# A flamingo block (gated cross-attention, then a mixture of experts) on one core: the last batch's softmax sums moved by fp32 products, routing waits and tables rearranged

## What is computed

```python
x = x + tanh(g_xattn[0]) * xattn(layernorm(x), ctx, Wq, bq, Wk, bk, Wv, bv, Wo, bo)
x = x + tanh(g_ffn[0]) * ffn(layernorm(x), gate_w, w1, w2, w3)
# xattn: q, k, v = W @ x + b over channels; per head softmax(q k * SCALE) v; then Wo @ out + bo
# ffn:   logits = x @ gate_w.T; top 2 of softmax; sum of w2 (silu(w1 x) * (w3 x)) * weight
```

## Time and profile before

| | us |
|---|---|
| median of 3 runs (775.40 to 776.07) | 775.88 |
| the profiled execution's own time | 774.61 |
| its span, first to last instruction | 772.9 |

### The profile page before, as it was taken

One profiled execution on the slowest core, in us unless ns is written; L12 is line 12 of the kernel. 1 busy time (PEld: TensorE's weight loads), 2 busy tenths in 40 slices (PEclk: granted clock), 3 DMA queues, 4 the chain that ended last, 5 costly groups with the idle time before them and its releaser, 6 DMA issues.

```text
span 772.9 us, 14065 instructions
## 1 busy us (share of the span) xinstructions
PE 636.8 (82%) x4313; PEld 298.2 (39%) x4314; DVE 414.1 (54%) x765; ACT 328.7 (43%) x395; POOL 227.0 (29%) x176
## 2 busy tenths in 40 slices
PE   8397599998989999899774130399999999999992
PEld 6321022322323233233112020366666666666661
DVE  5464658577695867766394555753333343334330
ACT  2076468576766857677761000022222222222220
POOL 3321124123242231421010020523334445444331
PEclk9789689899998999999986555599999999999997
DMA  7739668587776868868677636737777777755433
GB/s 248 243 105 348 187 196 282 160 286 244 227 231 195 291 193 265 271 188 277 203 221 221 201 117 237 260 107 190 199 200 190 190 196 210 197 105 92 82 42 42
DMA packets 64436, 153.44 MB, mean 199 GB/s; under 512 B 8261, under 2 KB 13894, under 8 KB 62854
## 3 DMA queue, kind: packets, MB, share of 16 engines
q1 hardware_dynamic: 44848, 98.58, 37.9%
q0 software_dynamic: 9632, 22.55, 15.4%
q10 hardware_dynamic: 9910, 31.75, 13.3%
HBM read 92.04 MB, written 58.46 MB: 195 GB/s over the span
## 4 chain that ended last, share of the span: by engine, by line
PE 43%; DMA 25%; DVE 13%; issue 8%; SPq 5%; POOL 4%; ACT 1%; POOLq 0%; DVEq 0%; ACTq 0%
PE S L1463 16%; PE O L1484 9%; DMA weight_parts<-wp 8%; DMA residual<-x 5%; PE O L1318 4%; DMA out<-yo,slot_out 4%; DMA q_parts<-qs 3%; PE S L1279 3%; PE MA L1358 2%; DVE wp L877 2%; PE S L1450 2%; PE MA L1379 2%; DMA zl<-osum 2%; PE MC L1358 2%; DVE wp L879 2%
## 5 line engine op out<-in xcount | busy, mean ns | idle before, releaser
L769 ACT ACTIVATE prob<-S 128x1024 f32<-128x1024 f32 x256 | 254.2, 1025 | 144.7 <-PE S L1279 113.1
L1463 PE MATMUL S<-W,xT 128*128 x1032 | 148.7, 301 | 1.2 <-DVE xT L1219 1.2
L1318 PE MATMUL O<-prob,V 128*32 128x512 f32 x1024 | 147.4, 650 | 0.0
L1279 PE MATMUL S<-Q,K 48*128 48x512 f16 x512 | 101.5, 411 | 35.4 <-ACT prob L769 25.3
L1463 PEld LDWEIGHTS S<-W,xT 128*128 128x128 f16 x1032 | 99.6, 98 | 38.4 <-issue 1.4
L687 POOL DMA_INDIRECT out<-yo,slot_out x43 | 68.6, 1594 | 119.5 <-ACT yo L819 78.8
L1279 PEld LDWEIGHTS S<-Q,K 48*128 48x128 f16 x512 | 24.0, 94 | 182.3 <-ACT prob L769 110.8
L1484 PE MATMUL O<-W,hT 128*128 (+1 forms) x344 | 90.3, 381 | 0.9 <-DVE hT L1239 0.9
L1227 DVE SCALAR_TENSOR_TENSOR hh<-S,act 128x320 f32<-128x320 f32 x43 | 21.1, 492 | 122.0 <-PE S L1463 122.0
L879 DVE SCALAR_TENSOR_TENSOR wp<-wf,wp 128x1024 f16<-128x1024 f32 x48 | 69.7, 1452 | 1.7
L877 DVE TENSOR_SCALAR wp<-wf 128x1024 f16<-128x1024 f32 x48 | 41.4, 862 | 37.4 <-DMA weight_parts<-wp 37.4
(11 more groups left out here) (171 smaller groups left out, 675.5 us busy)
## 6 DMA issues: line engine op xcount, KB each, us to landing
wf<-wall ACTq DMA_DIRECT2D x48, 512.0 KB, 6.5
weight_parts<-wp SPq DMA_DIRECT2D x46, 512.0 KB, 7.3
W<-weight_parts SPq DMA_DIRECT2D x10, 2048.0 KB, 10.1
K<-k_parts SPq DMA_DIRECT2D x8, 1024.0 KB, 11.7
Q<-q_parts SPq DMA_DIRECT2D x8, 1024.0 KB, 7.7
k_parts<-ks SPq DMA_DIRECT2D x24, 256.0 KB
q_parts<-qs SPq DMA_DIRECT2D x24, 256.0 KB
ctx<-ctx_in SPq DMA_DIRECT2D x8, 512.0 KB, 8.2
```

The costliest lines, as they stand in the source:

```text
L769: act.activation(prob[:, u % RING, :], S[u % 2][:, :], ACT.Exp, scale=SCALE).then_inc(g.exp, 1)
L1279: last = pe.matmul(S[u % 2][:, s * T:(s + 1) * T], K[par][r0:r0 + rows_, 2 * g4 + n, st * P:(st + 1) * P], Q[par][r0:r0 + rows_, 2 * g4 + ...
L1318: last = pe.matmul(O[g4 % 2][2 * DK * j:2 * DK * (j + 1), :], V[par][:, st, head(g4, j), :], prob[:, u % RING, (j % 2) * T:(j % 2 + 1) * T ...
L1463: last = pe.matmul(ps, xT[par][:, xp * TT + k, :], W[:, bass.ds(off + (w * WCOL + (2 * k + n) * F), F)], start=(k == 0 and (xp, w) == (0, 0)),
```

## The change

It does six things.

1. For batch 7 alone, the sums no longer go through DRAM. POOL writes four 0/1 matrices into the idle tile `cs` in slot 8 (`pick`, one memset and four copies). PE multiplies `osum` by them: DEN spreads the sums over their values' rows, NUM moves the second half of the values (`shared`; two fp32 products of 128x512 each). For the first half of the channels (m=0) the sums are spread at step 11 of slot 8, into MA; DVE inverts all 512 columns at once and `over_sums` moves the values by four smaller DMAs. For m=1 both products run at the start of slot 9, into S0. The bounds are still tested on `zl`, which four small DMAs now fill.
2. The logits of batch 6 move from step 15 of slot 8 to slot 9, behind these products; the best two of 12 groups are taken in slot 8, of four after `both_runs`. `bad` is made after batch 7's product; PE waits for it before o1. In slot 9 statistics, inverse spread and normed x go half by half, and the two copies to `xT2` stand ahead of the fp16 part of x.
3. In all slots the first half of `lg` waits only for the copy of t0, and its second half for t1.
4. Quarters: five in slots 6 and 7 (a new one at step 9), nine in slot 8 (none at 7 and 11, one at 14), one in slot 9, four in FFN tiles.
5. DVE no longer waits for PE's `s_done` nor for the store of the tokens (POOL waits for that). ACT and SP wait, for each expert, only for its own quarters; ACT's wait for `osum` ends with slot 8's DMAs.
6. The weighted tables are made by DVE: the first behind `row_hot`, the second behind `table`. The FFN loop writes out 7 tiles instead of 3 ahead of its rounds.

```diff
@@ quarters @@
+        STEPS = {0: (), 1: (1, 3, 5, 7, 9, 11, 13, 14), 2: (2, 7, 12, 14),
+                 3: (2, 7, 12, 14), 4: (2, 7, 12, 14), 5: (2, 7, 12, 14),
+                 6: (2, 7, 9, 12, 14), 7: (2, 7, 9, 12, 14), 8: (0, 2, 4, 6, 9, 10, 12, 13, 14),
+                 9: (2,)}
-            elif t.i is None and t.add == B:
-                steps = (0, 2, 4, 6, 7, 9, 10, 11, 12, 13)
-            elif t.i is None and t.add == B + 1:
-                steps, first = (2, 2, 10, 10), At(None, 0, QUARTERS - 6)
@@ tiles @@
-            first = TR - 1
+            first = 2 * TR - 1
@@ sync: slot @@
-                    if c:
-                        bc = t.before(2)
+                    bc = t.before(2)
+                    if c and not b_:
+                        wait(sp, g.os, bc, GROUPS, GROUPS)
+                        last_sums(1)
+                    elif c:
...
-                    else:
+                    elif b_:
                         weights(0, 9)
+                        sp.wait_ge(g.os, GROUPS * (B - 1) + 2)
+                        sp.wait_ge(g.on, B)
+                        last_sums(0)
+                        weights(9, 10)
...
+                        if b_ and not a:
+                            sp.wait_ge(g.zl, 16 * (B + 1))
+                            sp.wait_ge(g.shared, 1)
+                            for j in range(GH):
+                                over_sums(j, osum[1 - par], 1)
+                            weights(10, 13)
                         wait(sp, g.x2l, bc, 1, 1, s_bog)
...
-                    weights(10 if a else 9, VS)
+                    weights(10 if a else 13 if b_ else 0, VS)
@@ scalar: experts 0 and 1 @@
-                act.wait_ge(g.oz, OZ * B + 16)
+                act.wait_ge(g.oz, OZ * (B - 1) + OZ_LAST + 16)
...
-            for n in range(2):
-                act.wait_ge(s_wst[n], 16 * (2 * NE - 1))
             for e in range(EB // 2):
+                for n in range(2):
+                    act.wait_ge(s_wst[n], 16 * 2 * (e + 1))
@@ vector: the last slot @@
+                def last_normed():
+                    of = osum[(B - 1) % 2]
+                    dve.wait_ge(g.oz, OZ * (B - 1) + OZ_LAST + 16)
+                    dve.wait_ge(g.rz, B)
+                    dve.tensor_tensor(on[:, 0, :], of[:, 0, :], zc[:, 0, :], ALU.mult).then_inc(g.rz, 1)
+                    dve.wait_ge(g.rz, B + 1)
+                    dve.tensor_copy(os_[:, 0, 0, :], on[:, 0, :]).then_inc(g.rz, 1)
+                    dve.wait_ge(g.rz, B + 2)
+                    dve.tensor_tensor(os_[:, 1, 0, :], on[:, 0, :], os_[:, 0, 0, :], ALU.subtract).then_inc(g.rz, 1)
+                    dve.wait_ge(g.shared, 2)
+                    dve.reciprocal(zc[:, 1, :], S[0][:, 0:T]).then_inc(g.rz, 1)
+                    if not guard:
+                        dve.wait_ge(g.zl, 16 * (B + 3))
+                        bounds(At(None, 0, B - 1))
...
+                    dve.wait_ge(g.shared, 3)
+                    dve.wait_ge(g.rz, B + 4)
+                    dve.tensor_tensor(on[:, 1, :], S[0][:, T:2 * T], zc[:, 1, :], ALU.mult).then_inc(g.on, 1)
+                    dve.wait_ge(g.c_full, NCU * (B - 1))
+                    logits_out(At(None, 0, B - 2))
...
+                        if last_b and v == DEN_AT:
+                            dve.wait_ge(g.shared, 1)
+                            dve.reciprocal(zc[:, 0, :], MA[:, :]).then_inc(g.rz, 1)
+                            best(g.best, 0, NT - 2 * CT)
@@ vector: routing @@
-            dve.sem_inc(s_done, 1)
-            dve.wait_ge(s_done, 2)
-            best(s_best, NT - CT, NT)
+            best(s_best, NT - 2 * CT, NT)
...
+            weighted(0, w_hi)
             dve.wait_ge(s_tab, 1)
...
+            weighted(1, w_lo)
             dve.wait_ge(s_tab, 2)
...
-                if j.i is None and j.add < 2:
+                if j.i is None and j.add < 4:
-                    split_quarter(At(None, 0, QUARTERS - 2 + j.add))
+                    split_quarter(At(None, 0, QUARTERS - 4 + j.add))
@@ tensor @@
-                    wait(pe, g.c_free, b, NCU, 1 + {"o0": 0, "o1": 0, "t0": 1, "t1": 2, "lg": 4}[name])
+                    wait(pe, g.c_free, b, NCU, 1 + {"o0": 0, "o1": 0, "t0": 1, "t1": 2, "lg": 3}[name])
...
                         for m in range(CT):
+                            wait(pe, g.c_free, b, NCU, C_USES["t0"] + 2 + m)
...
+                def shared(into, of0, of1, m):
+                    pe.wait_ge(g.sel, 5)
+                    for n, of in enumerate((of0, of1)):
+                        pe.wait_ge(g.os, GROUPS * (B - 1) + 2 * m + 1 + n)
+                        last = pe.matmul(into, picked(of), osum[(B - 1) % 2][:, CT * n + m, :], start=(n == 0), stop=(n == 1))
+                    last.then_inc(g.shared, 1)
...
+                        shared(S[0][:, 0:T], DEN0, DEN1, 1)
+                        shared(S[0][:, T:2 * T], NUM0, NUM1, 1)
+                        output(At(None, 0, B - 2), "lg", a)
...
+                        if last_b and v == DEN_AT:
+                            pe.wait_ge(g.c_free, NCU * (B - 2) + 2)
+                            shared(MA[:, :], DEN0, DEN1, 0)
+                            if last_b and what == "t0":
+                                pe.wait_ge(g.rz, B)
```

198 lines of the change are left out of this document (120 added, 78 removed).

## The result

The changed kernel takes **754.61 us** (median of 4 runs, 751.13 to 756.48); the kernel before, 775.81 (4 runs, 775.4 to 776.07). The medians are 21.2 us apart. The ratio is 0.9708, with a 95% interval of 0.9658 to 0.9758 (22.7 us by it). The prediction said 750.2 us, 743 to 760, which is 25.7 us less. The profiled execution, the fastest of the four, took 751.13 us with a span of 749.4.

A forecast was written before the change was run, and what follows sets the result against it. It took PE to bound the FFN stage, but slots 8 and 9 and the routing to be held by waits for stores, transfers and exp. Terms summed to -25.7 us: 750.2 us against the median of 775.88, range 743 to 760.

The forecast's parts named there:

- Logits in two halves, slots 2 to 6: Logits product's first half fits PE's idle time, next step starts 1.0 us earlier in five slots: -5.0 us, bounds -5 and 0.
- rival 1: DVE becomes slot 8's bound (+2.2 us); next x load halves the two-halves gain (+2.5): 757.4 us; chance 0.18.
- Two quarters more, slots 6 and 7: Each extra quarter adds 1.9 us of DVE work, partly hidden in its waits: +1.5 us, bounds 0 and +3.8.
- Slot 8: Step 11's wait for a store goes; DVE's own work is late next: -2.5 us, from gain 4.2 to loss 2.2.
- Slot 9: Last `osum` copy to last logits, 36.0 us before, takes 23.1: -12.9 us, bounds -15 and -10.
- From the logits to the exp's use: Routing behind the logits, 13.8 us before; first expert load is issued earlier: -4.8 us, bounds -6.8 and 0.
- Rival 2: Expert load late behind 2 MB of stores, ACT's exp 4.8 us later, that gain 0: 755.0 us; chance 0.12.
- Tables: Routing tables on DVE without POOL beside them, first weighted table added: -3.9 us, bounds -4.6 and +3.
- tables to first tile: `slot_tok` to first FFN tile, 7.2 us before, 9.1 with DVE's second weighted table: +1.9 us, bounds +0.5 and +3.
- Rival 5: FFN stage: PE held at half its clock behind a stage with less idle time: 983 us if throughout; chance 0.01.
- Rival 3: Reciprocal at 8.6 ns a column, 1.0 us more in each of two places: 752.2 us; chance 0.05.
- Rival 4: PE stays at the upper clock through slot 9 and stores are quick, -2 and -2: 746.2 us; chance 0.04.

The follow-up runs named there:

- whole_lg: Changed kernel, with the logits product waiting for both copies again in all slots: 755.62 us, 0.9668 of the kernel before.
- x_early: Changed kernel, with SP loading the next slot's x right behind the transfer into `zl` (slot 1: at its start): 739.44 us, 0.953 of the kernel before.
- before_x_early: Kernel before the change, with only the load of the next slot's x issued early: 764.11 us, 0.9841.
- the second copy: The changed kernel measured and profiled once more, nothing edited: 752.1 us, 0.9685 of the kernel before.
- four_quarters: Changed kernel, with four quarters in slots 6 and 7 and six in FFN tiles: 759.26 us, 0.9774 of the kernel before.
- before_exp_first: Kernel before the change, with ACT computing the routing's exp ahead of its expert loads: 771.97 us, 0.9936.
- pool_tables: Changed kernel, with the two weighted tables made by POOL again: 753.05 us, 0.9737 of the kernel before.

## Why the prediction was right, and where a step failed

**Right in the sum.** The kernel came out 4.4 us above the forecast in the median, inside its range. The forecast case was the likeliest one and it is what happened, with one of its terms paid out in small part. That the sum came as near as this is partly luck: set against the profiled execution, slots 2 to 7, the way to the first tile and the FFN stage fell short by 5.0 us with the start, and slots 8 and 9 and the exp's use gave 2.7 us more than forecast. The largest term, slot 9, rests on the rows of two profiles; no run takes its parts (products in place of transfers, half by half, fewer quarter stores ahead) one by one. And the prediction's 0.2% for what a measurement can tell was too fine: the ten executions of the changed kernel lie between 749.7 and 756.5 us.

- *Logits in two halves, slots 2 to 6: -5.0.* This is the step that failed. "PE's next step starts 1.0 us earlier" is true of PE, whose idle time ahead of the product over slots 1 to 7 fell from 8.6 to 1.3 us. It was priced as if PE set the pace of a slot. The profile gives -1.6 us for four slots and -1.2 for slots 2 to 6 (232.4 to 231.2, the fifth quarter of slot 6 included), nearly the prediction's own sign of being wrong ("if slots 2 to 6 are not shorter"); ten profiles give some -2 for four slots, and the whole time tells no difference (`whole_lg`). What set the pace was the next x: `x_early` and `before_x_early` show what its wait was worth, 12.7 and 11 us. DVE's wait for it went from 8.6 to 15.7 us in the first profile and to 10.3 in the second, so that this wait took up the halves' gain is likely and not shown. The prediction named it as the bound of 0 and as half of rival 1, and weighed it too low. DVE's 8.6 us for x stand in the trace of before, and the page's chain of work that ended last gives "DMA residual<-x 5%": four loads of 9.4 to 11.1 us in slots 3 to 6, 40.9 us in all. The prediction makes no use of either.
- *Two quarters more, slots 6 and 7: +1.5.* The two slots are 1.4 us longer, and 2.4 in the second copy, with the last of the halves' gain in them; `four_quarters` has them at 87.0 us, 0.9 and 1.9 less than the two copies. Consistent with +1.5.
- *Slot 8: -2.5.* Measured -2.8, and -1.1 in the second copy. (The prediction's own steps give 2.2 for the case that it describes.) The second stand is gone, DVE's own work and PE's wait for the reciprocal took its place. Step 14's split waited 0.70 us for its store, where 2.2 were reckoned. Rival 1's slot 8 did not come.
- *Slot 9: -12.9.* Measured -13.7, 22.3 us in place of 23.1. Two sizes were off, in opposite directions: POOL's power of one column takes 0.57 us, where the two-column 1.74 was taken as the most, and DVE stood 1.95 us for `zl`, which was in the bounds only.
- *From the logits to the exp's use: -4.8.* Measured -6.4, 0.4 short of the bound of -6.8. The first load was issued at 437.57 and had landed when the second, which waits for it, was issued at 446.2, before anything needed it; the +3 for sharing the DMA engines was not paid by it. Rival 2 fell. `before_exp_first` shortens this stage by 6.2 us with exp's place alone.
- *Tables: -3.9, tables to first tile: +1.9.* Measured -4.0 and +2.4. Both mechanisms are shown by `pool_tables`. The second term is bounded twice: the weights' product is done at 473.7, and the gathered rows come at 474.4 and are turned at 475.5, with a DMA share of 0.84 from an expert load beside them. In the second copy they came at 477.9, and the stage took 10.9 us.
- *FFN: 0.* +0.9, and -0.8 in the second copy. The difference between the two is the first tile (5.99 and 4.84 us), both entered at a clock of 0.50: scatter. Rival 5, the clock held down all through, did not come: 0.99.
- *Reciprocal of 512 columns: 3.4 us.* Measured 3.35, twice. The Trainium skill ("VectorE: DVE Perf Modes", "First, the fixed hardware budget") read as a repeat count of 8 gave 4.3, as an estimate. The trace does not agree with that reading. Rival 3 fell with it.
- Rival 4, PE at the upper clock all through slot 9, fell too: the mean was 0.72.

## What to carry to other kernels

Before an engine's earlier start is priced as a gain, list every wait of the loop's other engines for the thing that ends it: an 8.6 us wait row for a load on a queue that nobody had shortened was worth more than the work saved, and moving one DMA issue by some 10 to 13 us gave 12.7 us. The chain of work that ended last named the load before any edit was made. And compare a stage in several executions before a difference of 1 or 2 us gets a cause: the first tile took 4.75 to 6.37 us with no edit that touched it. When the order on a DMA queue is written by hand, a load whose destination is free has no reason to stand behind stores that wait. And a split or copy that is "hidden in a tile" stays hidden only while its buffer's older store lands in time; at the fifth quarter it had not, and PE, two engines on, paid for it.
